# Latent attention: the probabilities' low halves subtracted one bank at a time, with scores and value products waiting for their own bank

## The reference, cut to what matters

```
q = rms(x) @ Wq; kv_latent, k_rope = split(rms(x) @ Wkva)
att = q . [kv, rope(k_rope)] / sqrt(64); causal mask
p = softmax(att); y = p @ kv; y @ Wo
```

## Time and profile before

| | us |
|---|---|
| median of three runs | 2640.64 |
| lowest and highest run | 2635.53, 2642.32 |
| the profiled execution, its own time | 2641.81 |
| span of the profiled execution | 2640.0 |
| TensorE, matmuls busy | 2412.7 (91% of the span) |
| VectorE busy | 1796.9 (68%) |
| ScalarE busy | 1348.8 (51%) |

### The profile page before, as it was taken

How to read it: one execution, slowest core, us unless ns; L and a number is a source line. 1 busy time by engine, 2 the same in 40 slices (tenths; PEclk the granted TensorE clock), 3 DMA queues, 4 the chain that set the end, 5 groups by cost and what they waited for, 6 DMA issues and landing times. The chain is left out here.

```text
span 2640.0 us, 45233 instructions
## 1 busy us (share of the span) xinstructions
PE 2412.7 (91%) x16852; PEld 1983.4 (75%) x16852; DVE 1796.9 (68%) x3056; ACT 1348.8 (51%) x2031; POOL 927.3 (35%) x1046
## 2 busy tenths in 40 slices
PE   7999868999999999999999969999768888999998
PEld 5777655777777777777777758888657776888887
DVE  6888864886778767876777646666466657666664
ACT  5666533766666666665666733333234434332322
POOL 1233333464446354645444331212346641001000
PEclk8999988999999999999999979999879998999999
DMA  4011114433343334333433243332301104121221
GB/s 140 27 35 52 30 39 124 123 104 105 98 137 101 104 105 143 96 101 102 134 109 106 62 131 103 102 105 74 110 26 35 35 29 132 44 75 35 81 57 41
DMA packets 193802, 223.80 MB, mean 85 GB/s; under 512 B 37400, under 2 KB 157232, under 8 KB 189936
## 3 DMA queue, kind: packets, MB, share of 16 engines
q1 hardware_dynamic: 191792, 220.38, 28.3%
q10 hardware_dynamic: 1792, 0.53, 0.1%
HBM read 150.95 MB, written 55.73 MB: 78 GB/s over the span
## 5 line engine op out<-in xcount | busy, mean ns | idle before, releaser
L1240 DVE TENSOR_REDUCE l_negmax<-l_mx 128x1 f32<-128x512 f32 (+3 forms) x608 | 394.4, 654 | 131.7 <-PE l_mx L1637 130.5
L1486 ACT ACTIVATE l_Phi<-l_s 128x1024 fp32r<-128x1024 f32 x288 | 295.1, 1025 | 182.5 <-PE l_s L1659 176.0
L1252 DVE TENSOR_TENSOR l_Plo<-l_s,l_Phi 128x1024 fp32r<-128x1024 f32 x288 | 350.1, 1216 | 15.5 <-ACT l_s L1490 15.1
L1670 PE MATMUL l_o<-l_Phi,l_V 128*128 128x256 f32 x1152 | 307.0, 288 | 6.6 <-ACT l_Osb L1498 2.3
L1657 PE MATMUL l_s<-l_QA,l_KK 128*128 128x512 f32 x576 | 280.3, 487 | 27.2 <-DVE l_Plo L1252 23.5
L1670 PE MATMUL l_o<-l_Plo,l_V 128*128 128x256 f32 x1152 | 300.2, 282 | 0.0
L1490 ACT ACTIVATE l_s<-l_s 128x1024 f32<-128x1024 f32 x288 | 295.0, 1024 | 0.0
L2786 ACT ACTIVATE m_hidhi<-m_h 128x512 fp32r<-128x512 f32 x168 | 106.2, 632 | 359.5 <-DVE m_h L2635 359.5
L1637 PE MATMUL l_mx<-l_KK,l_QA 128*128 128x512 f32 (+3 forms) x768 | 271.7, 394 | 6.5 <-DVE l_negmax L1240 2.7
L1670 PEld LDWEIGHTS l_o<-l_Phi,l_V 128*128 128x128 f32 x1152 | 219.6, 191 | 40.4 <-issue 29.1
L1659 PE MATMUL l_s<-l_QB,l_KL 65*128 65x512 f32 x576 | 229.3, 398 | 0.0
(11 more groups left out here) (469 smaller groups left out, 6383.9 us busy)
## 6 DMA issues: line engine op xcount, KB each, us to landing
l_qd<-l_qs SPq DMA_DIRECT2D x256, 128.0 KB, 2.4
l_QA<-l_qd SPq DMA_DIRECT2D x64, 512.0 KB, 3.5
l_QB<-l_qd SPq DMA_DIRECT2D x64, 256.0 KB, 4.3
l_R<-l_rd SPq DMA_DIRECT2D x128, 128.0 KB, 2.9
m_spread<-m_combs SPq DMA_DIRECT2D x62, 256.0 KB, 5.1
m_spread<-m_combs SPq DMA_DIRECT2D x124, 128.0 KB, 4.9
xs<-next_store SPq DMA_DIRECT2D x32, 256.0 KB, 2.0
l_rps<-l_rp SPq DMA_DIRECT2D x128, 64.0 KB, 1.9
```

Of the source, the lines that this page charges most:

```text
L1240: v.tensor_reduce(negmax[:, n % 2, at + h0:at + h1], piece_of(number, chunk), AX.X, ALU.max, negate=True).then_inc(reduced, 1)
L1252: v.tensor_tensor(Plo[:, s % 3].rearrange("p u h q -> p (u h q)"), S2[s % 2][:, :], Phi[:, s % 3].rearrange("p u h q -> p (u h q)").bitcas ...
L1486: a.activation(Phi[:, s % 3].rearrange("p u h q -> p (u h q)"), S2[s % 2][:, :], ACT.Exp, scale=L_D ** -0.5).then_inc(exped, 1)
L1670: mm = pe.matmul(O[:, odd * 2 * P:(odd + 1) * 2 * P].rearrange("p (j q) -> p j q", j=2), V[:, b % 2, k, 64 - 64 * odd:192 - 64 * odd], src ...
```

## The change

The subtraction becomes two instructions of one bank (512 columns) each, each raising `lowered` by one. `score(u)` now waits at every u from 4 on, with the value u - 3, which is the subtraction of unit u - 4, the one that last read this bank. `weigh(u)` waits for u + 1, its own unit's subtraction. What `low` itself waits for is as before, and only its first half carries the waits.

```diff
                 v.wait_ge(exped, 2 * s + 2)
                 if s >= 3:
                     v.wait_ge(weighed, 2 * s - 4)
-                v.tensor_tensor(Plo[:, s % 3].rearrange("p u h q -> p (u h q)"), S2[s % 2][:, :],
-                                Phi[:, s % 3].rearrange("p u h q -> p (u h q)").bitcast(F32), ALU.subtract)\
-                    .then_inc(lowered, 1)
+                for x in range(2):
+                    v.tensor_tensor(Plo[:, s % 3, x].rearrange("p h q -> p (h q)"),
+                                    S2[s % 2][:, x * HALF:(x + 1) * HALF],
+                                    Phi[:, s % 3, x].rearrange("p h q -> p (h q)").bitcast(F32), ALU.subtract)\
+                        .then_inc(lowered, 1)
...
-                if u % 2 == 0 and s >= 2:
-                    pe.wait_ge(lowered, s - 1)
+                if u >= 4:
+                    pe.wait_ge(lowered, u - 3)
...
-                pe.wait_ge(lowered, s + 1)
+                pe.wait_ge(lowered, u + 1)
```

## The result

| | before | after |
|---|---|---|
| median of five runs, us | 2640.64 | 2615.10 |
| lowest to highest | 2635.53 to 2644.17 | 2612.28 to 2622.74 |
| span of the profiled execution | 2640.0 | 2613.7 |
| stage, second matmul of the first score to the last value product | 1086.3 | 1061.4 |

The ratio is 0.9911 with a 95% interval of 0.9898 to 0.9923: 23.5 us faster by the ratio, where 17.6 were forecast (2623). The stage accounts for 24.9 of the 26.3 us between the two spans.

What follows compares the result with a forecast made beforehand. TensorE, 96% busy, was taken as the bound; 6.7 + 0.6 + 17.4 + 0.3 - 1.2 - 2.9 - 0.3 - 2.5 = 18 us off 2641.8 gave 2623.8, set at 2623; range 2608 to 2635.

Steps and rivals of the forecast that it cites:

- The mechanism: Scores of even u: the first half, 687 ns, releases them 0.53 us earlier; 39 us over 107 waits before later caps.
- The waits left: Score waits on the subtraction fall from 51.7 to about 12 us, nearly all in slot 4 and unbroken runs.
- The second half's 0.08: On VectorE a pair of halves takes 0.08 us more than one subtraction, 23 us in all, free where a gap follows.
- Rival 3: VectorE becomes the bound: 0.16 more for each pair, 46 us on the path, +14, 2655 us; chance 0.07.
- The cap in slot 4: The weigh there waits for the evacuation of `O`; 29 waits losing 16.8 us can give only 6.7.
- Its sign: Idle time before the value products' weight loads at L1670 rises by some 7 us, evacuations 0.14 before the weigh.
- Rival 1: All capped waits go, evacuation and maxima's row moving forward too: 39 us won, 2601 to 2602; chance 0.10.
- The second wait at odd step starts: A step's first score, also waiting for the maxima's row, pays for a second wait: 2.5 us, bounds 0 and 5.
- The row of maxima: At eight odd steps, 2.9 us of slot 7's stalls only moves to the first score's wait for the maxima's DMA.
- So 0.35 us is lost where the weight loads show 0.40: Idle time before held scores' weight loads slightly overstates the loss: the 107 waits, 51.7 us, lose 46 us.

Runs made afterwards that it cites:

- the first two experiments: Subtraction in halves: with scores and value products waiting for both halves, 1.0017 to the kernel before; with only value products waiting for both, 0.9905.
- quarters: Four subtractions of 256 columns instead of two of 512, scores and value products waiting by bank: 0.9927 to the kernel before, 2615 us.
- another edit, The fourth experiment: Kernel before, unsplit, with the subtraction issued ahead of the query's subtraction and the reductions in slot 2 of even steps: 0.9964, 9.5 us faster.
- the first experiment: Subtraction in two instructions, but scores and value products wait for both halves of a pair: 1.0017 to the kernel before, 4.5 us slower.

## Why the prediction was right, and where a term was off

**The mechanism.** As predicted: the half is 681 ns and the score of even u is released half a microsecond earlier. That the gain is this release, and not the shorter instructions or the value products' waits, is shown by the first two experiments. No score of odd u waits for the subtraction; the three at which the profile names it are the ones above. The waits left are 12.2 us, as forecast.

**The second half's 0.08.** The two take 1.28 to 1.29 us where the one took 1.22, so it is 0.07. By itself it costs 4.5 us, under the 9 that 107 waits of 0.08 make. Rival 3 had 46 us of VectorE's time on the path, and nothing like it shows, with halves or with quarters. The section of the Trainium skill that the prediction names for it (VectorE: DVE Perf Modes, "The DRAIN you can't avoid") goes on to say that a next operation that is not held starts earlier. The trace agrees with this second sentence: the second half starts 0.60 or 0.61 after the first, which takes 0.68, in all 288 pairs.

**The cap in slot 4.** As predicted, and shown twice: taking the slot's waits away by another edit gave 9.5 us for 18.5 us of waits, and nothing measurable on top of the halves. Its sign came out larger than forecast: some 7 us more of idle time before the value products' weight loads were expected, and they show 18 more (31.6 before, 49.3 after), while the matmul rows themselves show 8 more. Rival 1, which denied the cap, falls.

**The second wait at odd step starts.** I took 2.5 us, from a wrong reading of the earlier trace rows. The 0.17 there is a wait for the subtraction, to which the profile gives no releaser:

```profile
710.31 1.22 DVE L1252 TENSOR_TENSOR l_Plo<-l_s,l_Phi 128x1024 fp32r<-128x1024 f32 x1
```

It ends at 711.52 and the weight load starts 0.12 later, at 711.64. So it is at all eight such step starts. In the first experiment, where the pair is finished 0.07 later, there are twelve, of 0.18 to 0.26, with the same 0.12. What the second wait adds shows in the run without the row's waits, unsplit: at the five of the eight starts that then wait for the subtraction alone, the load follows it by 0.05. So 0.06 is the price of the second wait, and only where the subtraction comes last. After the change no step start but the stage's very first has idle time of this kind. The term is 0, and the eight waits, which I had not counted among the 107, gave back 1.3 us (0.16 each, by the matmuls' distance).

**The row of maxima.** I took 2.9 us. The waits went from 5.4 to 14.7 us, 9.3 more, three times what I took. I had counted only steps that this row already held; eight of these nine still are, and eleven others have come to it. Whether all of it is a loss stays open, as said above; the sum below takes it so.

**The term that was missing.** "So 0.35 us is lost where the weight loads show 0.40" stopped at the first matmul. A held score also loses the cover of its second weight load. Before the change, behind the unheld score at 1013.06 of the earlier trace rows and then around the held one at 1014.60:

```profile
1013.07 0.19 PEld L1659 LDWEIGHTS l_s<-l_QB,l_KL 65*128 65x128 f32 x1
1013.30 0.40 PE L1659 MATMUL l_s<-l_QB,l_KL 65*128 65x512 f32 x1
...
1014.60 0.19 PEld L1657 LDWEIGHTS l_s<-l_QA,l_KK 128*128 128x128 f32 x1 [0.40 <-DVE l_Plo L1252]
...
1014.71 0.19 PEld L1659 LDWEIGHTS l_s<-l_QB,l_KL 65*128 65x128 f32 x1
1014.94 0.39 PE L1659 MATMUL l_s<-l_QB,l_KL 65*128 65x512 f32 x1
```

Unheld, the second load runs under the first matmul and the second matmul starts 0.24 after it. Held, the first load begins with its matmul, the second follows 0.11 later, and the matmul starts 0.34 after the first. There are 313 scores without a mask right behind a value product. Of these, those that start late fell from 109 to 33 (held by whatever), with a mean distance of 0.34 against 0.24 for the others: 76 x 0.10 = 7.6 us. With a mask ahead the distance is 0.42 held or not. The fourth experiment, whose expectation already held this term, agrees: the cap alone leaves 7 us, with 0.10 for each of 31 scores it is 10, and 9.5 was measured. Its interval of 3 us to either side does not exclude the 7.

**The sum again.** 18 + 2.5 (no cost of the second wait) + 1.3 (waits at step starts) + 7.6 (weight loads) - 6.4 (row of maxima) = 23 us. The timed runs show 23.5, the stage 24.9, or about 20 without the clock's share. They can't be told apart more finely than 3 us, so the sum is not proved term by term. The forecast came as near as 6 us in part by luck: 11.4 us that it had left out or taken off stand against 6.4 that it had taken too small. What was off is the sizing of a wait's loss; the mechanism, the cap and the sign held.

## What to carry to other kernels

A long instruction that frees several buffers at once can be cut so that each is freed when it is done; read the price of the shorter instruction from a row of that size, and count the gain only as far as the next wait in the same slot. Go through each wait with the distance of the next dependent instruction to its own releaser: where that distance is already the smallest one in the trace, the wait removed will only be waited there. Before a DMA with a wait is moved forward on a compute engine's list, look at what stands behind it. Before two traces are set against each other, look at the granted clock in each stretch: a difference of 10 us at the lower level is worth 4 or 5 us here.

## What the runs showed of the hardware that was not expected

- A matmul held by a semaphore costs more than its wait: the next weight load, no longer covered, adds 0.10 us (0.34 against 0.24 between two matmuls of 512 columns).
- A score's weight load starts 0.05 us after the subtraction that releases it; where it also waits for the row of maxima, 0.12 (eight step starts). Where the subtraction does not come last, the second wait costs nothing: 30 of the 32 odd step starts stand 0.12 behind the last value product, as before the change.
- Stalls of TensorE came with stretches of the lower clock. With the DMA one slot sooner it had 1.2 GHz for 75 us of the stage, against 10 in the changed kernel. An estimated 29 us of this run's loss are put down to it.
- VectorE reads one bank while TensorE writes the other bank of the same PSUM tensor: 681 ns for 512 columns, not more than the 687 of the earlier trace rows.
